# The attention's output product moves to another accumulator bank, and the attention's end is reordered, in a decoder layer on one core

## The chip, the core and the metric

The kernel runs on one core of one Trainium2 chip. A core has a matrix engine (TensorE, "PE" in the rows, with its weight loads as "PEld"), a vector engine (VectorE, "DVE"), a scalar engine (ScalarE, "ACT"), a general one (GpSimd, "POOL") and a queue that mostly starts DMAs (SyncE, "SP"). Each works through its own list of instructions in order, and they meet at semaphores. TensorE writes only into PSUM, which has eight banks of 128 partitions by 512 fp32 numbers; here each bank is a named buffer, `bank0` to `bank7`. The metric is the device time of one execution in microseconds (us); lower is better.

## What is computed

One layer of a decoder in fp32 on x of 4 sequences, 512 tokens and 512 channels: x plus attention of its layer norm, then x plus a product with a context quantised to fp8 steps, then x plus a mixture of experts with one shared expert.

```python
x = x + attention(layernorm(x), wq, wk, wv, wo)   # 32 heads of 64, 8 key heads, rotary, causal softmax
x = x + cross(layernorm(x), ctx)                  # both rounded to e4m3 steps, einsum 'emk,enk->emn'
x = x + moe(layernorm(x), Wg, W1, W3, W2, sw1, sw3, sw2)  # 8 experts, top 1, capacity 256, plus a shared one
```

The matrix products run in fp32 accuracy as three products of a high and a low part (`three`: high times high, high times low, low times high).

## The kernel before

The first two thirds of the time are one loop, `for h in range(NH + 7)`, that every engine runs in its own version. NH is 128: 32 units (4 batches times 8 key groups) of 4 heads. In what follows a step is one pass of this loop, and the number behind a helper is the head it works on. In step h TensorE does, in this order: `scores(h, 3)` and `scores(h, 2)`; two thirds of the step's `project` (the query, key and value products of two units later, into banks 6 and 7); `weigh(h - 3)` (turned weights times values, into bank 5); `turn_p(h - 2, 0)` into bank 2; `scores(h, 1)`; `turn_p(h - 2, 1)` into bank 3; in every fourth step `turn_v` (four small transposes); `scores(h, 0)`; `turn_p(h - 2, 2)` into bank 4; the last third of `project`; and `attn_out(h - 7)`, the product of one finished token tile of the attention with wo, six matmuls into bank 5. `turn_p` is the transpose of the softmax weights P. It fills banks 2, 3 and 4, and each of these is read twice: ScalarE rounds it to the high part PTh (`pt_hi`, L887), then VectorE subtracts that to get the low part PTl (`pt_lo`, L1260).

Bank 5 has two users. `weigh` leaves its sum there; ScalarE copies the lower half out (`lower_out`, Otmp, L881) and VectorE adds the two halves (`join`, Opair, L1254). After that `attn_out` may write the bank. VectorE then adds the result to X (`attn_out` on VectorE, L1269), and the next `weigh` waits for this addition (`v_x`). The rule stands in `wait_bank5`.

VectorE's step is: `inverse_sums(h - 1)` (L1208); in some steps one or two extras (maxima of the context at L1292, quantisation steps, the low part of new weights); `masked(h, 3)` and `masked(h, 2)`, which scale and mask 512 and 384 columns of scores (L1219); a key or value piece; `masked(h, 1)`; `join(h - 3)`; `pt_lo(h - 2, 0)`; `masked(h, 0)`; `pt_lo(h - 2, 1)` and `pt_lo(h - 2, 2)`; a rotary product in most steps (L1232); and the addition for `attn_out(h - 7)` at the very end. ScalarE does the exponentials (L875), `lower_out`, `pt_hi` and `pair`; GpSimd divides the weights by their sums (L1660) and makes low parts.

From step SIDE = NH - 11 = 117 on, the work of the next stages is laid in between: a table made by `slots()` gives for each slot number s a list of stages (`plan(s, stage, b, i)` for batch b and tile i). Slots -44 to -9 lie in steps 117 to 134, two in a step; slots -8, -7 and -6 behind the loop; and slots from -5 on in front of the matmuls of the feed-forward part, `ffn(x, k)` with x = 0 to 7 for the shared expert and k = 0 to 7, so that slot 8x + k - 5 comes before `ffn(x, k)`. From `attn_out(117)` on the bank is 7 in place of 5. The stages of a batch run: statistics (`stats2`), scale and bias (`norm2`), a normed copy (`look`), its maxima (`peaks`), `scales`, `scaled`, rounding on VectorE and GpSimd (`cross_round`), transpose (`cross_turn`), product (`cross_product`), then statistics, norm and transpose again (`stats3`, `rstd3`, `norm3`, `route_turn`), and `logits`, `choose` and `place`. The feed-forward weights come as pieces of 256 KB through a ring of six buffers RW; `split_piece` splits each into high and low. Behind the loop `wait_attention` makes an engine wait until the whole attention is done. It stands before the load of the router's weights (Graw) and of two small tables, before the clearing of the tiles Gh and Gl made from them, and before the first `ffn`.

## Time and profile before

| | us |
|---|---|
| median of three runs | 1531.93 (1531.92 to 1536.74) |
| the profiled execution | 1532.62 |
| its span, first to last instruction | 1530.8 |
| mean granted TensorE clock | 0.990 of full speed |

Busy time of the engines over the span: TensorE 1437.9 us (94%), VectorE 1147.5 (75%), GpSimd 1027.0 (67%), ScalarE 984.9 (64%). The sum of a busy engine's rows can exceed the time, because a matmul's end is modelled and overlaps the next one's start; so what a wait costs TensorE is read here from one start to the next. A matmul of 512 columns starts 0.23 us after the one before it when nothing is waited for. Step h = 8 of the attention's loop starts at 98.9 us, step 50 at 408.0, step 120 at 951.6 and step 127 at 1012.5; the first matmul of the feed-forward part is at 1049.0.

### The profile page before, as it was taken

The page shows a single profiled execution, that of the slowest core. Times are in us where ns is not written, and L with a number is a line of the kernel's source. Part 1 is how long each engine was busy: PE and PEld are TensorE (multiplying, and loading weights), DVE is VectorE, ACT ScalarE, POOL GpSimd, SP SyncE. Part 2 cuts the span into 40 slices and gives each one's busy share as a digit, 9 for nine tenths or more (in the row PEclk, how much of TensorE's full clock was granted, in tenths as well). Part 3 has the DMA queues.
Part 4 walks back from the last instruction along what each step waited for, and adds up shares of the span by engine and source line. Part 5 has one row for each costly group of instructions (what it writes and reads, how often), then busy time and mean ns, then how long its engine had stood idle before and what let it go on. Part 6 is the DMA issues. An engine that isn't in the chain of part 4 may idle for free.

```text
span 1530.8 us, 26938 instructions
## 1 busy us (share of the span) xinstructions
PE 1437.9 (94%) x8617; PEld 1259.0 (82%) x8617; DVE 1147.5 (75%) x2820; ACT 984.9 (64%) x2509; POOL 1027.0 (67%) x1043
## 2 busy tenths in 40 slices
PE   5899999999999999999999999897898999999997
PEld 3778888888878888778888888776787888999996
DVE  7678888887887887887888788787565754677773
ACT  4687786777776887878878787756141412555562
POOL 3787888888877788888898888644404131366663
PEclk9999999999999999999999999999999999999998
DMA  6445454334322424334234342504111011587772
GB/s 209 116 122 166 124 147 134 87 111 124 84 80 63 112 75 128 88 83 123 73 113 126 82 132 66 169 1 147 43 35 49 22 43 39 170 267 236 253 244 80
DMA packets 108620, 174.74 MB, mean 114 GB/s; under 512 B 20936, under 2 KB 42696, under 8 KB 108480
## 3 DMA queue, kind: packets, MB, share of 16 engines
q1 hardware_dynamic: 104448, 160.51, 36.0%
q0 software_dynamic: 3840, 12.25, 2.1%
q8 instruction: 70, 1.15, 0.3%
q14 instruction: 70, 0.57, 0.1%
q10 hardware_dynamic: 192, 0.26, 0.1%
HBM read 94.05 MB, written 33.18 MB: 83 GB/s over the span
## 4 chain that ended last, share of the span: by engine, by line
PE 66%; ACT 12%; DVE 11%; issue 5%; DMA 2%; POOL 2%; SPq 1%; DVEq 0%; POOLq 0%; ACTq 0%
PE bank L484 15%; PE bank L486 14%; PE bank L485 14%; PE bank L536 5%; ACT P L875 5%; PE bank L551 4%; PE bank L552 3%; PE bank L502 3%; PE bank L503 3%; DVE P L1219 2%; ACT PTh L887 2%; PE bank L476 2%; ACT Otmp L881 2%; DVE PTl L1260 1%; DVE Opair L1254 1%
## 5 line engine op out<-in xcount | busy, mean ns | idle before, releaser
L875 ACT ACTIVATE P<-P,mn 128x512 f32<-128x512 f32 (+3 forms) x512 | 284.5, 557 | 206.9 <-DVE mn L1219 203.1
L1660 POOL TENSOR_TENSOR P<-P,ri 128x128 f32<-128x128 f32 (+3 forms) x512 | 360.7, 737 | 30.7 <-DVE ri L1208 30.7
L1219 DVE CUSTOM_DVE_ANT_0 P<-bank,mask 128x512 f32<-128x512 f32 (+3 forms) x512 | 236.6, 480 | 84.3 <-PE bank L503 82.8
L1260 DVE TENSOR_TENSOR PTl<-bank,PTh 128x512 fp32r<-128x512 f32 (+1 forms) x384 | 229.8, 599 | 34.1 <-ACT PTh L887 31.1
L536 PE MATMUL bank<-ident,P 128*128 128x128 f32 x1280 | 202.6, 273 | 2.5 <-POOL P L1660 2.5
L887 ACT ACTIVATE PTh<-bank 128x512 fp32r<-128x512 f32 (+1 forms) x384 | 198.1, 517 | 3.9 <-PE bank L536 1.0
L502 PE MATMUL bank<-KT,QT 128*128 128x256 f32 (+2 forms) x512 | 188.1, 368 | 6.4 <-DVE mn L1219 6.4
L484 PE MATMUL bank<-XT,Wh 128*128 128x512 f32 x384 | 163.8, 427 | 8.1 <-DVE XT L1190 3.5
L503 PE MATMUL bank<-KT,QT 128*128 128x256 f32 (+2 forms) x512 | 166.0, 324 | 0.0
L551 PE MATMUL bank<-PTh,VS 128*128 128x256 f32 (+2 forms) x512 | 161.1, 326 | 5.2 <-DVE X L1269 2.4
L552 PE MATMUL bank<-PTl,VS 128*128 128x256 f32 (+2 forms) x512 | 154.5, 324 | 0.0
L486 PE MATMUL bank<-XT,Wl 128*128 128x512 f32 x384 | 152.9, 398 | 0.0
L485 PE MATMUL bank<-XT,Wh 128*128 128x512 f32 x384 | 152.6, 397 | 0.0
L536 PEld LDWEIGHTS bank<-ident,P 128*128 128x128 f32 x1280 | 150.1, 141 | 3.0 <-POOL P L1660 3.0
L1698 POOL TENSOR_TENSOR OTl<-Opair,OTh 128x512 fp32r<-128x512 f32 x64 | 83.6, 1306 | 94.7 <-ACT OTh L958 93.9
L484 PE MATMUL bank<-Oh,OTh 128*128 128x512 f32 x256 | 106.0, 414 | 20.9 <-DVE Opair L1254 15.5
L1254 DVE TENSOR_TENSOR Opair<-bank,Otmp 64x512 f32<-64x512 f32 x128 | 87.4, 683 | 39.8 <-ACT Otmp L881 38.5
L502 PEld LDWEIGHTS bank<-KT,QT 128*128 128x128 f32 x512 | 96.8, 189 | 21.2 <-DVE mn L1219 8.9
L1011 ACT ACTIVATE hm<-bank 128x256 f32<-128x256 f32 x96 | 36.4, 379 | 117.8 <-PE bank L486 117.0
L551 PEld LDWEIGHTS bank<-PTh,VS 128*128 128x128 f32 x512 | 96.2, 188 | 19.4 <-issue 6.7
L503 PEld LDWEIGHTS bank<-KT,QT 128*128 128x128 f32 x512 | 97.5, 190 | 10.5
L552 PEld LDWEIGHTS bank<-PTl,VS 128*128 128x128 f32 x512 | 96.1, 188 | 10.0
(225 smaller groups left out, 4090.2 us busy)
## 6 DMA issues: line engine op xcount, KB each, us to landing
RW<-in_wf SPq DMA_DIRECT2D x153, 256.0 KB, 3.4
QT<-qh SPq DMA_DIRECT2D x256, 64.0 KB, 2.0
QT<-ql SPq DMA_DIRECT2D x252, 64.0 KB, 2.0
Oraw<-in_wo SPq DMA_DIRECT2D x16, 512.0 KB, 4.8
KT<-KT SPq DMA_DIRECT2D x32, 256.0 KB, 3.0
Wraw<-in_wqkv SPq DMA_DIRECT2D x9, 768.0 KB, 4.7
xnx<-in_ctx SPq DMA_DIRECT2D x24, 256.0 KB, 3.5
saved<-Wh SPq DMA_DIRECT2D x7, 768.0 KB, 3.5
```

Source lines behind the costliest of these rows:

```text
L484: e.matmul(ps, lh, rh, start=start, stop=False)
L485: e.matmul(ps, lh, rl, start=False, stop=False)
L486: return e.matmul(ps, ll, rh, start=False, stop=stop)
L502: e.matmul(ps[:, 0:k], lhs, KT[:, u % 2, 0, 0:k], start=True, stop=False)
L503: e.matmul(ps[:, 0:k], lhs, KT[:, u % 2, 1, 0:k], start=False, stop=True).then_inc(p_s, 1)
L536: last = e.transpose(ps[:, tokens(m)], src, ident[:, :])
L551: e.matmul(ps[:, q:512], lhs, pt_of(PTh, kb), start=kb == 0, stop=False)
L552: last = e.matmul(ps[:, q:512], lhs, pt_of(PTl, kb), start=False, stop=kb == 3)
L875: e.activation(pq, pq, ACT.Exp, bias=mn[:, z, qb:qb + 1], scale=-1.0, accum_out=rs[:, z, qb:qb + 1]).then_inc(a_exp, 1)
L1219: e.tensor_tensor_reduce(P[:, z, off[qb]:off[qb] + k], bank[n % 2][:, 0:k], mask[:, 512 - k:512], -0.125, BIG, ALU.add, ALU.min, mn[:, z, ...
L1260: e.tensor_tensor(pt_part(PTl, part), bank[2 + part][:, 0:128 * n].rearrange("p (m n) -> p m n", n=128), pt_part(PTh, part).bitcast(F32), ...
L1660: e.tensor_tensor(pq, pq, ri[:, z, qb:qb + 1].to_broadcast([128, n]), ALU.mult).then_inc(g_norm, 1)
```

## The change

Three things are changed.

1. The bank of `attn_out`. `attn_out(n)` for n below 117 writes bank 2, which it shares with `turn_p(., 0)`, in place of bank 5. TensorE waits there for both readers of `turn_p(h - 2, 0)` in that bank. The addition to X moves on VectorE from the end of step h to step h + 1, behind `masked(h + 1, 3)` and `masked(h + 1, 2)`, and `turn_p(h - 1, 0)` in step h + 1 waits for it. `weigh` now waits for `join` alone. The first transposes of batches 2 and 3 (`first_turn` in steps 52 to 59) move from bank 2 to bank 5. From `attn_out(124)` on the outputs alternate between banks 7 and 2.
2. The table. Batch 1's statistics go to slots -44 to -38, its scale to a short start on VectorE and 14 small instructions on GpSimd, its `look`, `peaks`, `scales`, `scaled` and rounding up to six slots earlier, its `cross_turn` and `cross_product` one slot earlier. Batch 0's `logits`, `choose` and `place` go from slots -2, 0 and 3 to -6, -4 and -2. GpSimd's part of `place` is a stage of its own, `scatter`, in the old slots.
3. The end of the loop. The router's weights and tables are loaded in step 125, their tiles are made in steps 128 to 130, the pieces' loads start a step earlier, eleven pieces are split in steps 128 to 133 in place of eight in steps 131 to 134, an activation that brings in the Silu table runs in step 129, and most uses of `wait_attention` become waits for just the bank or tile that is needed.

```diff
+    plan(-6, "logits", 0)
+    plan(-4, "choose", 0)
+    plan(-2, "place", 0)
+    plan(3, "scatter", 0)
+    for i in range(TB):
+        plan(-44 + 2 * i, "stats2", 1, i)
+        plan(-14 + i, "look", 1, i)
+        at = (-4, -3, -1, 1)[i]
+        plan(at, "cross_round", 1, i)
+        plan((-1, 0, 1, 3)[i], "cross_turn", 1, i)
...
+        pieces_at = {NH: 2, NH + 1: 2, NH + 2: 1, NH + 3: 2, NH + 4: 2, NH + 5: 2}
...
+        def out_bank(n):
+            return bank[2 if n < NH - 11 or n >= NH - 4 and n % 2 else 7]
...
-        def wait_bank5(need, h, user):
-            if user == "attn_out":
-                need.wait_ge(a_tmp, h - 2)
-                need.wait_ge(v_join, h - 2)
-            elif h < 8 or h - 8 >= NH - 11:
-                need.wait_ge(a_tmp, h - 3)
-                need.wait_ge(v_join, h - 3)
-            else:
-                need.wait_ge(v_x, h - 7)
+        def wait_bank5(need, h):
+            if 53 <= h < 61:
+                wait_xt(need, h - 44)
+            else:
+                need.wait_ge(a_tmp, h - 3)
+                need.wait_ge(v_join, h - 3)
...
             def turn_p(h, part):
-                if part == 0 and 51 <= h < 59:
-                    wait_xt(need, h - 42)
+                if part == 0 and 0 <= h - 6 < NH - 11:
+                    need.wait_ge(v_x, h - 5)
...
             def attn_out(n):
-                ps = bank[7 if late else 5][:, :]
+                ps = out_bank(n)[:, :]
                 if not late:
-                    wait_bank5(need, n + 7, "attn_out")
+                    need.wait_ge(a_pt, 3 * (n + 5) + 1)
+                    need.wait_ge(v_pt, 3 * (n + 5) + 1)
                 elif n == NH - 11:
                     wait_part(need, NU - 1, 2)
-                else:
+                elif n <= NH - 4:
                     need.wait_ge(v_x, n)
+                else:
+                    need.wait_ge(a_pt, 3 * NH)
+                    need.wait_ge(v_pt, 3 * NH)
+                    need.wait_ge(v_x, n - 1)
...
                     if x == 0 and k < 3:
-                        wait_attention(need)
+                        need.wait_ge(a_pt, 3 * NH)
+                        need.wait_ge(v_pt, 3 * NH)
+                        need.wait_ge(a_tmp, NH)
+                        need.wait_ge(v_join, NH)
+                        if k == 2:
+                            need.wait_ge(v_x, NH)
...
# VectorE's loop
                     masked(h, 3)
                     masked(h, 2)
+                if 0 <= h - 8 < NH - 11:
+                    attn_out(h - 8)
...
-                if 0 <= h - 7 < NH:
+                if NH - 11 <= h - 7 < NH:
                     attn_out(h - 7)
...
# the DMA queue's loop
-                if h == NH - 2:
+                if h == NH - 3:
+                    need.wait_ge(g_bq, len(jobs))
+                    e.dma_start(Graw[:, :, :], wg_in).then_inc(d_k, 16)
+                    e.dma_start(rank[:, :], rank_in).then_inc(d_k, 16)
+                    e.dma_start(tri[:, :], tri_in).then_inc(d_k, 16)
                     for _ in range(NR):
                         load_piece()
```

How the moved instructions stand can be seen in three places. The line numbers behind L are those of each version of the file. On TensorE, first, the end of a step in the middle of the attention, before (`ident,P` into bank 4 is `turn_p(h - 2, 2)`, `XT0,Wh` is `project`, `Oh,OTh` is `attn_out`, `KT,QT` the next step's scores):

```order
L536 MATMUL bank4<-ident,P 128x128 x2
L484 MATMUL bank6<-XT0,Wh 128x512
L485 MATMUL bank6<-XT0,Wh 128x512
L486 MATMUL bank6<-XT0,Wl 128x512
L484 MATMUL bank5<-Oh,OTh 128x512 [waits v_join,a_tmp]
L485 MATMUL bank5<-Ol,OTh 128x512
```

The same place after:

```order
L563 MATMUL bank4<-ident,P 128x128 x2
L511 MATMUL bank6<-XT0,Wh 128x512
L512 MATMUL bank6<-XT0,Wh 128x512
L513 MATMUL bank6<-XT0,Wl 128x512
L511 MATMUL bank2<-Oh,OTh 128x512 [waits v_pt,a_pt]
L512 MATMUL bank2<-Ol,OTh 128x512
```

Nothing has moved in TensorE's list here: the bank and the semaphores are other ones. On VectorE, one step from the join on, before (`Opair` is `join`, `PTl` is `pt_lo`, the ISA rows with `mask` are `masked`, `X<-X,bank5` is the addition):

```order
L1254 TENSOR_TENSOR Opair<-bank5,Otmp 64x512 [waits a_tmp]
L1260 TENSOR_TENSOR PTl<-bank2,PTh 128x512 [waits p_pv,a_pt]
L1219 ISA P,mn<-bank1,mask 128x128 [waits p_s]
L1219 ISA mn 128x1
L1260 TENSOR_TENSOR PTl<-bank3,PTh 128x4x128 [waits a_pt]
L1260 TENSOR_TENSOR PTl<-bank4,PTh 128x2x128 [waits a_pt]
L1269 TENSOR_TENSOR X<-X,bank5 128x512 [waits v_x,p_ao]
L1208 RECIPROCAL ri<-rs 128x4 [waits a_exp]
L1292 TENSOR_REDUCE wam<-xnx 128x4 [waits d_by0]
L1219 ISA P,mn<-bank0,mask 128x512 [waits p_pt,p_s]
L1219 ISA mn 128x1
L1219 ISA P,mn<-bank1,mask 128x384 [waits p_s]
```

And after:

```order
L1294 TENSOR_TENSOR Opair<-bank5,Otmp 64x512 [waits a_tmp]
L1300 TENSOR_TENSOR PTl<-bank2,PTh 128x512 [waits p_pv,a_pt]
L1259 ISA P,mn<-bank1,mask 128x128 [waits p_s]
L1259 ISA mn 128x1
L1300 TENSOR_TENSOR PTl<-bank3,PTh 128x4x128 [waits a_pt]
L1300 TENSOR_TENSOR PTl<-bank4,PTh 128x2x128 [waits a_pt]
L1248 RECIPROCAL ri<-rs 128x4 [waits a_exp]
L1332 TENSOR_REDUCE wam<-xnx 128x4 [waits d_by0]
L1259 ISA P,mn<-bank0,mask 128x512 [waits p_pt,p_s]
L1259 ISA mn 128x1
L1259 ISA P,mn<-bank1,mask 128x384 [waits p_s]
L1259 ISA mn 128x1
```

The addition has left the place behind the third `pt_lo` (it now follows the last row shown), and `join` and the first `pt_lo` stand in the same order as before. On the DMA queue, at the attention's end, before (`RW` are the feed-forward pieces, `Graw`, `rank` and `tri` the router's weights and tables):

```order
L1980 DMA RW<-in_wf 128x512 [waits v_piece,a_piece]
L1980 DMA RW<-in_wf 128x512 [waits g_piece,a_piece]
L2083 DMA Graw<-in_wg 128x32 [waits v_x,g_o,a_o,p_ao]
L2084 DMA rank<-in_rank 128x8
L2085 DMA tri<-in_tri 128x128
```

And after:

```order
L2132 DMA Graw<-in_wg 128x32 [waits g_bq]
L2133 DMA rank<-in_rank 128x8
L2134 DMA tri<-in_tri 128x128
L2035 DMA RW<-in_wf 128x512 [waits d_keep]
L2035 DMA RW<-in_wf 128x512 x5
```

Before, the three tables are loaded behind fourteen pieces and the wait for the whole attention; now they are ahead of the first piece.

## Rows read from the trace of the kernel before

**Rows 1.** The page's head and its busy line of TensorE

```profile
span 1530.8 us, 26938 instructions
...
PE 1437.9 (94%) x8617; PEld 1259.0 (82%) x8617; DVE 1147.5 (75%) x2820; ACT 984.9 (64%) x2509; POOL 1027.0 (67%) x1043
```

**Rows 2.** Windows: stretch, length, busy us (count) by engine, granted clock, DMA share, GB/s

```profile
600.00:950.00 350.00, 339.23 (x1919) 289.59 (x1917) 284.13 (x756) 280.94 (x754) 305.63 (x322) 1.00 0.37 98
...
1020.00:1050.00 30.00, 23.44 (x126) 19.15 (x126) 25.49 (x58) 14.38 (x27) 11.00 (x10) 0.94 0.27 84
1050.00:1083.00 33.00, 24.53 (x161) 22.65 (x160) 24.18 (x51) 20.49 (x49) 17.98 (x22) 0.90 0.33 95
```

**Rows 3.** Waits, 105 to 960 us: us in total, times, longest

```profile
PE bank L484 <- DVE Opair L1254: 13.7, 26, 1.2
...
PE bank L502 <- DVE mn L1219: 2.9, 4, 1.2
...
PE bank L551 <- DVE X L1269: 1.2, 2, 0.9
```

**Rows 4.** Timeline of TensorE, steps 49 and 50: start us, us, instruction

```profile
404.37 0.60 PE L536 MATMUL bank<-ident,P 128*128 128x128 f32 x4
404.72 0.36 PE L502 MATMUL bank<-KT,QT 128*128 128x256 f32 x1
...
406.62 0.39 PE L484 MATMUL bank<-Oh,OTh 128*128 128x512 f32 x1
...
411.84 0.36 PE L502 MATMUL bank<-KT,QT 128*128 128x256 f32 x1
...
413.74 0.39 PE L484 MATMUL bank<-Oh,OTh 128*128 128x512 f32 x1
```

**Rows 5.** Timeline of VectorE, the same two steps

```profile
403.12 0.09 DVE L1219 DVE_READ_ACCUMULATOR2_ANT mn<- 128x1 f32 x1
...
405.24 0.42 DVE L1219 CUSTOM_DVE_ANT_0 P<-bank,mask 128x256 f32<-128x256 f32 x1 [1.52 <-PE bank L503]
...
405.59 0.68 DVE L1254 TENSOR_TENSOR Opair<-bank,Otmp 64x512 f32<-64x512 f32 x1
406.20 0.67 DVE L1260 TENSOR_TENSOR PTl<-bank,PTh 128x512 fp32r<-128x512 f32 x1
...
412.82 0.68 DVE L1254 TENSOR_TENSOR Opair<-bank,Otmp 64x512 f32<-64x512 f32 x1
413.54 0.69 DVE L1260 TENSOR_TENSOR PTl<-bank,PTh 128x512 fp32r<-128x512 f32 x1
```

**Rows 6.** Timeline of TensorE, step 109, the wait in front of attn_out

```profile
874.42 0.40 PE L486 MATMUL bank<-XT,Wl 128*128 128x512 f32 x1
875.79 0.47 PE L484 MATMUL bank<-Oh,OTh 128*128 128x512 f32 x1 [0.97 <-DVE Opair L1254]
```

**Rows 7.** Timeline of VectorE, step 109

```profile
874.96 0.68 DVE L1254 TENSOR_TENSOR Opair<-bank,Otmp 64x512 f32<-64x512 f32 x1 [1.16 <-ACT Otmp L881]
875.58 0.69 DVE L1260 TENSOR_TENSOR PTl<-bank,PTh 128x512 fp32r<-128x512 f32 x1
```

**Rows 8.** Timeline of TensorE from the last attn_outs to batch 1's product

```profile
1042.11 0.50 PE L484 MATMUL bank<-Oh,OTh 128*128 128x512 f32 x1 [1.11 <-DVE X L1269]
1046.05 0.50 PE L484 MATMUL bank<-Oh,OTh 128*128 128x512 f32 x1 [2.28 <-DVE X L1269]
1049.01 0.36 PE L484 MATMUL bank<-XT,Uh 128*128 128x256 f32 x1 [1.31 <-issue]
...
1059.22 0.47 PE L484 MATMUL bank<-XT,Gh 128*128 128x512 f32 x1 [1.52 <-issue]
...
1073.61 1.08 PE L476 MATMUL bank<-ident,work 128*128 128x128 f32 x4 [5.48 <-POOL work L1707]
...
1080.43 0.47 PE L484 MATMUL bank<-XT,YT 128*128 128x512 f32 x1 [1.47 <-ACT YT L964]
```

**Rows 9.** Timeline of ScalarE, the router's tables and the wait for their load

```profile
1057.17 0.23 ACT L1113 ACTIVATE Gh<-Graw 128x32 fp32r<-128x32 f32 x1 [2.19 <-DMA tri<-in_tri]
...
1058.42 1.28 ACT L1011 ACT_TABLE_LOAD   x1
```

145 lines of the change are left out of this document (84 added, 61 removed).

## Prediction

> **What bounds the kernel now.** I read the head of the page first [rows 1]: TensorE is busy for 94% of the span, and no other engine for more than 75%. So a change can win only where TensorE waits, and it loses wherever it makes TensorE wait more. The windows say where it waits [rows 2]: in the attention's loop 339.2 of 350 us are busy, while in the 63 us from 1020 to 1083, where the attention ends and the feed-forward part begins, only 48.0 are. The waits of the loop [rows 3] name what the change aims at: `attn_out` (L484 with Opair as releaser) waits for the join in front of bank 5. The profile gives 13.7 us in 26 pieces, and leaves out what the modelled ends of the matmuls cover. From start to start (the start of `attn_out`'s first matmul, less the start of the matmul before it, less 0.23 us) I get 21.3 us over steps 8 to 116, counting every step. Smaller waits of the same stretch are the scores' wait for a mask and `weigh`'s wait for the addition to X, 4.1 us in the profile [rows 3] and 5.5 from start to start.
>
> **The new place of attn_out, step by step.** The change takes away the wait for the join, and puts a wait for both readers of bank 2 in its place. The second of these is `pt_lo(h - 2, 0)`, and on VectorE that stands directly behind the join. So the new release comes later than the old one, by one VectorE instruction, in every step. What that costs is the question, and a step without any lag shows it. In step 49 the join starts at 405.59 and the `pt_lo` at 406.20 with 0.67 [rows 5]: it ends at 406.87. TensorE starts 0.15 us after such an end (step 109: join 874.96 + 0.68 = 875.64, `attn_out` 875.79 [rows 6, 7]; with this 0.15 the join's ends give every wait of the 21.3 us within 0.02). So `attn_out` could start at 407.02, and it started at 406.62 [rows 4]: a wait of 0.40 in a step that had none. In step 50 it is 413.54 + 0.69 + 0.15 = 414.38 against 413.74 [rows 4, 5]: 0.64. The larger value is that of the steps whose join goes to the upper half of Opair, where neither join nor `pt_lo` overlaps its predecessor (0.72 from start to start, not 0.61).
>
> Can this wait shrink, once TensorE is later? No: its chain begins on TensorE. `scores(h, 1)` starts at 404.72, VectorE stands idle 1.52 us for it and starts the mask at 405.24, then come join, `pt_lo` and `attn_out` [rows 4, 5]. From these scores to `attn_out` TensorE has 1.90 us of work, the chain takes 2.30 to 2.54. A later TensorE moves both ends. Only the fourth kind of step, where `turn_v` puts 0.6 us more work in between, has 0.64 - 0.60 = 0.04 left. For the four kinds I take 0.04, 0.39, 0.64 and 0.50 (the last kind was 0.38 in clean steps and more behind extras), 42.4 us over the 109 steps.
>
> Where VectorE or ScalarE lag, the wait is longer. If `pt_lo` ended in each step where it ended before, the waits would sum to 79.6 us; in step 109 that is 875.58 + 0.69 + 0.15 - 874.65 = 1.77, where 1.14 was waited before. But two things relieve VectorE: the masks come 0.6 us earlier, as the addition no longer stands ahead of them, and each step leaves it at least the 0.4 above. So I take for each step the larger of its floor and its old wait: 49.0 us. **Term 1**: 49.0 - 21.3 = +27.7, from +21.1 (floors alone) to +58.3 (every end as before).
>
> **Term 2**, restarts: behind a wait the second matmul follows 0.31 us after the first in place of 0.23. Some 82 steps of 109 now wait where 45 did: 37 x 0.08 = +3.0.
>
> **Term 3**, waits that go: `weigh` for the addition and the scores for a mask that now comes earlier, -5.5 (0 to -8).
>
> **Term 4**, the addition behind the masks. Now `turn_p(h - 2, 0)` waits for it. The masks and the addition together end where the two masks ended before; in step 49 that is 403.12 + 0.09 = 403.21, plus 0.15, and `turn_p` starts at 404.37 [rows 4, 5], so 1.0 us is free. In about half of the steps, behind extras, nothing was free or up to half a microsecond too little (23.8 us of shortfall over 112 steps). Nearly all of it disappears because TensorE comes 0.4 to 0.8 us later from the step before. Were the wait of term 1 not there, it would be paid here. The first transposes in bank 5 put the same kind of wait in front of `weigh` in eight steps. Together +1 (0 to +5).
>
> **Term 5**, steps 117 to 123: four more statistics of 0.87 us each stand between join and `pt_lo`, and the old loop through bank 5 (weigh, join, attn_out, addition) is cut short in steps that have no `project` to hide anything. +2 (-3 to +6).
>
> **Term 6**, the end, is the gain. The outputs of tiles 126 and 127 waited for the addition before them, the single bank 7, and the first `ffn` for the last one: 1.20, 2.45 and 1.37 us from start to start [rows 8]. Two banks and the finer wait take these: -5.0. The router's product waited 1.5 us at 1059.22, for tiles whose tables were loaded behind the whole attention, which also held ScalarE for 2.19 us [rows 8, 9]; both loads now stand in step 125, and the Silu table's 1.28 us come early: -1.5. Batch 1's chain from `look` to `cross_turn` kept TensorE for 5.64 us at 1073.61, and 1.86 at 1080.43 [rows 8]. Behind the first it ran at the lower of its two clock levels, 1.2 GHz (24 matmuls 0.10 us late each, granted clock 0.90 of full in this window [rows 2]), another 2.4. With the chain six slots earlier and its product one slot earlier all of that should go: -9.9. New waits: `place` comes two slots behind `choose` in place of three, while VectorE's part of `choose` took 3.4 us, and the splits of the pieces fall on a VectorE that is 25.5 of 30 us busy there [rows 2]: +2.4. Sum -14 (-5 to -19).
>
> **The sum** is 27.7 + 3.0 - 5.5 + 1 + 2 - 14 = +14.2 us, on the profiled execution's 1532.62: 1546.8. That execution is 0.7 above the median of the runs, so I predict 1546.
>
> **Rules of the skill.** The gap that the change aims at is the same one in many steps, on the engine that should be saturated [rows 3]. The Trainium skill (Perfetto Trace Analysis, Optimization Strategy) says that such consistent bubbles can mean that there isn't enough PSUM for the next tile. By that rule another bank removes them, -21.3 in place of +27.7; the rows speak against it, since the bank that is given is free later than the old one. The Trainium skill also knows (TensorE: Matmul & The Clock Gate, A second HAM failure mode: psum-queue depth-cycling) that small idles between groups of matmuls, with banks cycled, can make the clock swing between its levels. The window from 600 to 950 us had waits up to 1.2 us, and its granted clock was 1.00 [rows 2, 3], so this trace doesn't show it.
>
> **The rivals.** *Not slower, because the bubbles go.* If VectorE's lag, and not the chain from the scores, sets join and `pt_lo` in nearly all steps, its 0.6 us of relief moves both ahead, and `attn_out` finds bank 2 free. Then terms 1 and 2 are -21.3 and -3, term 3 stays, term 4 is 0: 1532 - 21 - 3 - 5.5 + 2 - 14 = 1491. For it: half of the old waits are behind extras. Against it: the idle 1.52 us in front of the mask [rows 5], which says that VectorE waits for TensorE there. It decides where the floor falls under some 0.05 us a step; at half the floor the change would be about even. *Every `pt_lo` as late as before.* The relief goes nowhere, since ScalarE, busy without a gap in the lagging steps, sets the ends: term 1 is +58.3, and the sum +44.8, 1577. For it: in step 109 the join waited 1.16 us for ScalarE [rows 7]. *The end does not gain* because another wait stands behind each of the named ones: 1532.62 + 28.2 = 1561. *The clock swings*: six matmuls of `attn_out` at half rate in 82 steps, 6 x 0.2 x 82 = +98, about 1644. *Even*: the floor at its low end with all of the end's gain, 21.1 + 3 - 8 - 3 - 19 = -6, and somewhat more: 1527 to 1536.
>
> **How the numbers follow.** My forecast 0.60 (its own range 1532 to 1572), the bubbles go 0.14, every `pt_lo` as before 0.14, no gain at the end 0.05, even 0.05, the clock 0.02. A measurement of this kernel can tell about 0.3% from no change, 1527.3 to 1536.5. Faster is the first rival, 0.14. Same is the even case and the low edge of the forecast, 0.05 + 0.05 = 0.10. Slower is the rest, 0.76. The range leaves out the first rival, the clock, and the edges: 1527 to 1580.
>
> **What would show it.** If I am right, `attn_out` waits in three of four steps, released by PTl and not by Opair, for 45 to 60 us in all; a step of the early attention lasts 7.5 to 7.8 us where it lasted 7.12; there is no wait of `weigh` for X; `turn_p` hardly waits for X; and the first feed-forward matmul comes some 20 us later than 1049, followed by no gap of 5 us. I am wrong if step 50 or a step like it still takes 7.12 us, if the large wait is that of `turn_p` for X, or if the end of the kernel, from the first `ffn` on, isn't 8 us or more shorter than before.

## The result and the profile after

The change makes the kernel slower: 1584.49 us, the median of four runs (1582.49 to 1585.53), against 1532.66 (1531.92 to 1536.74) of the kernel before on the same chip. The ratio is 1.0335, with a 95% interval of 1.032 to 1.035. The prediction was 1546, with a range that ended at 1580: the sign is right, the size is not. The loss is 51.8 us where 14 were forecast. The profiled execution after spans 1580.4 us, 49.6 more than before.

The page's head and its line of TensorE, and two of its groups (the line of the operation, what it writes and reads, count | busy, mean ns | idle before it and the main releaser). They answer to [rows 1]:

```profile
span 1580.4 us, 27143 instructions
...
PE 1457.1 (92%) x8617; PEld 1260.5 (80%) x8617; DVE 1172.5 (74%) x2810; ACT 986.3 (62%) x2510; POOL 1026.7 (65%) x1057
...
L563 PE MATMUL bank<-ident,P 128*128 128x128 f32 x1280 | 205.0, 275 | 17.1 <-DVE X L1309 13.7
...
L511 PE MATMUL bank<-Oh,OTh 128*128 128x512 f32 x256 | 111.3, 435 | 43.6 <-DVE PTl L1300 41.7
```

In the changed kernel L511 is the first product of a group of three (L484 before), L563 is `turn_p` (L536), L578 `weigh` (L551), L1259 the mask (L1219), L1294 the join (L1254), L1300 `pt_lo` (L1260), L1309 the addition to X (L1269), L918 ScalarE's copy for the join (L881), L924 `pt_hi` (L887). TensorE does the same 8617 products. What is new are two waits: `attn_out` for PTl, 41.7 us, and `turn_p` for X, 13.7 us.

Where the 49.6 us lie, from start to start as in the prediction: 44.2 in steps 8 to 116 (830.9 us before, 875.1 after), 10.2 in steps 117 to 126 (82.7, 92.9), and -4.2 from step 127 to the end (518.3, 514.1), with -0.6 ahead of step 8. The waits of TensorE in steps 8 to 116, counted in the same way:

| in front of | before | after | forecast change | measured |
|---|---|---|---|---|
| attn_out (terms 1, 2) | 23.8 | 54.5 | +30.7 | +30.7 |
| scores and weigh (term 3) | 8.9 | 3.9 | -5.5 | -5.0 |
| turn_p (term 4) | 1.4 | 20.0 | +1 | +18.6 |

Here is `attn_out`'s wait in the profile, over the same steps. It answers to [rows 3]:

```profile
PE bank L511 <- DVE PTl L1300: 31.5, 79, 1.8
PE bank L563 <- DVE X L1309: 12.6, 14, 3.9
```

And here is one step of it, on TensorE and then on VectorE: step 50, the one whose wait the prediction worked out as 0.64 [rows 4, 5].

```profile
429.76 0.36 PE L529 MATMUL bank<-KT,QT 128*128 128x256 f32 x1
...
431.43 0.40 PE L513 MATMUL bank<-XT,Wl 128*128 128x512 f32 x1
432.30 0.47 PE L511 MATMUL bank<-Oh,OTh 128*128 128x512 f32 x1 [0.47 <-DVE PTl L1300]
```

```profile
430.28 0.42 DVE L1259 CUSTOM_DVE_ANT_0 P<-bank,mask 128x256 f32<-128x256 f32 x1 [1.32 <-PE bank L530]
...
430.75 0.69 DVE L1294 TENSOR_TENSOR Opair<-bank,Otmp 64x512 f32<-64x512 f32 x1
431.46 0.69 DVE L1300 TENSOR_TENSOR PTl<-bank,PTh 128x512 fp32r<-128x512 f32 x1
```

From `scores(h, 1)` at 429.76 to `attn_out` at 432.30 are 2.54 us, as the prediction's chain had it. VectorE still stands idle 1.32 us for the scores. TensorE starts 0.15 us after `pt_lo`'s end (432.15), and waits 432.30 - 431.43 - 0.23 = 0.64.

The other wait at its largest is in step 114. On VectorE, GpSimd and TensorE, in this order:

```profile
944.93 5.12 DVE L1366 TENSOR_SCALAR Zb<-Zb 128x512 f32<-128x512 f32 x1
949.98 0.68 DVE L1259 CUSTOM_DVE_ANT_0 P<-bank,mask 128x512 f32<-128x512 f32 x1
...
951.07 0.68 DVE L1309 TENSOR_TENSOR X<-X,bank 128x512 f32<-128x512 f32 x1
```

```profile
943.06 2.76 POOL L1701 TENSOR_TENSOR P<-P,ri 128x128 f32<-128x128 f32 x4
945.77 1.29 POOL L1784 TENSOR_TENSOR xnx<-xnx,Zb 128x512 f32<-128x512 f32 x1
947.02 2.75 POOL L1701 TENSOR_TENSOR P<-P,ri 128x128 f32<-128x128 f32 x4
949.73 1.45 POOL L1728 TENSOR_TENSOR KT<-kt,KT 64x512 fp32r<-64x512 f32 x1
```

```profile
951.89 0.63 PE L563 MATMUL bank<-ident,P 128*128 128x128 f32 x4 [3.86 <-DVE X L1309]
```

The operation on Zb is an extra that stands in front of the two large masks. It takes 0.40 us when nothing disturbs it. Here it took 5.12, while GpSimd worked without a gap. Masks, addition and `turn_p` stand behind it in a row.

The second largest is in step 79, where another extra, the look for a maximum, waits on VectorE for ScalarE. Before the change only masks stood behind it.

```profile
666.16 0.69 DVE L1346 TENSOR_REDUCE aam<-Wraw 128x4 f32<-128x512 f32 x1 [3.44 <-ACT Wraw L939]
```

```profile
668.68 0.63 PE L563 MATMUL bank<-ident,P 128*128 128x128 f32 x4 [2.84 <-DVE X L1309]
```

### The profile page after: what moved, and what is told of

Its sections match the earlier page's. It is cut to its first block, busy times and chain, and to the rows that moved or that the text cites. A ratio compares the mean times of both kernels' runs of the same rounds, so it can differ in the third digit from the quotient of the medians.

```text
span 1580.4 us, 27143 instructions
## 1 busy us (share of the span) xinstructions
PE 1457.1 (92%) x8617; PEld 1260.5 (80%) x8617; DVE 1172.5 (74%) x2810; ACT 986.3 (62%) x2510; POOL 1026.7 (65%) x1057
## 4 chain that ended last, share of the span: by engine, by line
PE 67%; DVE 16%; issue 7%; ACT 6%; DMA 2%; POOL 1%; SPq 1%; DVEq 0%; POOLq 0%; ACTq 0%
PE bank L511 16%; PE bank L512 14%; PE bank L513 14%; PE bank L563 5%; DVE PTl L1300 4%; PE bank L578 4%; PE bank L579 4%; PE bank L529 4%; PE bank L530 4%; DVE Opair L1294 3%; DVE P L1259 2%; PE bank L503 2%; ACT P L912 2%; ACT PTh L924 1%; DMA Oraw<-in_wo 1%
## 5 line engine op out<-in xcount | busy, mean ns | idle before, releaser
L1259 DVE CUSTOM_DVE_ANT_0 P<-bank,mask 128x512 f32<-128x512 f32 (+3 forms) x512 | 238.1, 483 | 140.8 <-PE bank L530 138.1
L1300 DVE TENSOR_TENSOR PTl<-bank,PTh 128x512 fp32r<-128x512 f32 (+1 forms) x384 | 228.7, 596 | 33.9 <-ACT PTh L924 31.6
L563 PE MATMUL bank<-ident,P 128*128 128x128 f32 x1280 | 205.0, 275 | 17.1 <-DVE X L1309 13.7
L924 ACT ACTIVATE PTh<-bank 128x512 fp32r<-128x512 f32 (+1 forms) x384 | 196.8, 514 | 3.6 <-PE bank L563 0.5
L511 PE MATMUL bank<-XT,Wh 128*128 128x512 f32 x384 | 163.7, 426 | 5.4 <-DVE XT L1230 2.9
L563 PEld LDWEIGHTS bank<-ident,P 128*128 128x128 f32 x1280 | 149.2, 142 | 22.5 <-POOL P L1701 14.5
L578 PE MATMUL bank<-PTh,VS 128*128 128x256 f32 (+2 forms) x512 | 160.3, 324 | 6.5 <-DVE PTl L1300 2.8
L511 PE MATMUL bank<-Oh,OTh 128*128 128x512 f32 x256 | 111.3, 435 | 43.6 <-DVE PTl L1300 41.7
L511 PEld LDWEIGHTS bank<-Oh,OTh 128*128 128x128 f32 x256 | 48.4, 189 | 92.5 <-ACT PTh L924 50.2
L578 PEld LDWEIGHTS bank<-PTh,VS 128*128 128x128 f32 x512 | 96.2, 188 | 17.8 <-issue 5.0
L918 ACT ACTIVATE Otmp<-bank 64x512 f32<-64x512 f32 x128 | 76.3, 596 | 49.2 <-PE bank L579 47.7
L530 PEld LDWEIGHTS bank<-KT,QT 128*128 128x128 f32 x512 | 98.1, 192 | 10.2
```

What stands on the lines that cost most here:

```text
L511: e.matmul(ps, lh, rh, start=start, stop=False)
L530: e.matmul(ps[:, 0:k], lhs, KT[:, u % 2, 1, 0:k], start=False, stop=True).then_inc(p_s, 1)
L563: last = e.transpose(ps[:, tokens(m)], src, ident[:, :])
L578: e.matmul(ps[:, q:512], lhs, pt_of(PTh, kb), start=kb == 0, stop=False)
L1259: e.tensor_tensor_reduce(P[:, z, off[qb]:off[qb] + k], bank[n % 2][:, 0:k], mask[:, 512 - k:512], -0.125, BIG, ALU.add, ALU.min, mn[:, z, ...
L1300: e.tensor_tensor(pt_part(PTl, part), bank[2 + part][:, 0:128 * n].rearrange("p (m n) -> p m n", n=128), pt_part(PTh, part).bitcast(F32), ...
```

## Experiments: which part costs

In the diffs, lines with - are of the kernel that is named and lines with + of the experiment. Every ratio is against runs of the kernel before on the same chip; compare these, and not the last microsecond of the medians.

**The new end alone.** The changed kernel with the bank part undone:

```diff
-            return bank[2 if n < NH - 11 or n >= NH - 4 and n % 2 else 7]
+            return bank[5 if n < NH - 11 else 2 if n >= NH - 4 and n % 2 else 7]
...
-                if 0 <= h - 8 < NH - 11:
-                    attn_out(h - 8)
...
-                if NH - 11 <= h - 7 < NH:
+                if 0 <= h - 7 < NH:
                     attn_out(h - 7)
```

> The changed kernel with the bank part undone: attn_out goes to bank 5 again behind the join, its addition stands at the end of the step, weigh waits for the addition, the first transposes use bank 2. The reordered end stays whole. Theory (the loss up to step 117, 43.7 us between the two traces, is all of the new bank and the moved addition; the end has its own balance): the time is 1532.7 plus what the end brings. If the 10.1 us lost in steps 117 to 127 are the end's own statistics and constants, 1532.7 + 10.1 - 4.2 = 1538.6; if they follow from the bank part, 1532.7 - 4.2 = 1528.5. By the prediction's terms 5 and 6 (-12) it would be 1520.7. Rival (the end's new order, by its other places on VectorE and ScalarE, costs the attention itself): step 117 starts well after the 929.8 us of before, and the time is over 1545.

Measured: 1531.7 us, ratio 0.9991 (0.9981 to 1.0001). Any gain or cost of the new end lies within the interval. Steps 117 to 126 take 87.4 us against 82.7, so 4.7 of the 10.2 us lost there are the end's own, and what comes later gives back as much.

**The bank part alone.** The kernel before with bank 2, the addition behind the masks, `turn_p`'s wait, and the first transposes in bank 5:

```diff
-                ps = bank[7 if late else 5][:, :]
+                ps = bank[7 if late else 2][:, :]
...
                     masked(h, 2)
+                if 0 <= h - 8 < NH - 11:
+                    attn_out(h - 8)
```

> The kernel before with the bank part alone: attn_out up to output 116 in bank 2, its addition behind the next step's two large masks, turn_p waiting for it, the first transposes in bank 5. Everything at the end as before. Theory (the bank part is the loss): step 117 starts some 43.7 us later than 929.8, and the time is 1532.7 + 43.7 = 1576; with the 10.1 us of steps 117 to 127, if these are its as well, 1586. Rival (half or more of the loss belongs to the end's order): below 1560.

Measured: 1584.5 us, ratio 1.0316 (1.0291 to 1.0342). This is the whole loss. Its trace has 46.1 us more than before in steps 8 to 116, and 5.5 more in steps 117 to 126 (88.2 us). With the 4.7 above this makes the 10.2.

## Experiments: bank, order and addition

Five kernels move three things one at a time: the addition's place, the place of `pt_lo(h - 2, 0)` on VectorE (in front of the join or behind it), and the place of `pt_hi(h - 2, 0)` on ScalarE (in front of the copy for the join or behind it). All have the new end and bank 2.

**The addition last.** In the changed kernel:

```diff
-                if 0 <= h - 8 < NH - 11:
-                    attn_out(h - 8)
...
-                if NH - 11 <= h - 7 < NH:
+                if 0 <= h - 7 < NH:
                     attn_out(h - 7)
```

> The changed kernel, attn_out in bank 2, but with its addition to X at the end of the step on VectorE, where the kernel before has it. Theory (turn_p's 20.0 us of wait come from the place behind the extras and the two masks, and nothing else hangs on it): turn_p's waits fall to under 2 us, attn_out's stay at 50 to 58, the scores wait some 3 to 4 us more for a mask, and the time is 1584.5 - 18.6 + 4 = 1570. Rival (the masks' 0.6 us of earliness is what keeps the join and pt_lo from coming still later): what turn_p gives back attn_out takes, its waits are 70 us or more, and the time is within 5 us of 1584.5.

**pt_lo first.** In the changed kernel:

```diff
-                if 0 <= h - 3 < NH:
-                    join(h - 3)
...
                 if 0 <= h - 2 < NH:
                     pt_lo(h - 2, 0)
+                if 0 <= h - 3 < NH:
+                    join(h - 3)
```

> The changed kernel with one swap on VectorE: pt_lo(h - 2, 0), which frees bank 2 for attn_out, stands in front of join(h - 3) and no longer behind it. pt_hi of the same bank ends 0.08 to 0.2 us behind the join's start in the trace after, so pt_lo can start some 0.6 us earlier in clean steps. Theory (the chain scores, mask, join, pt_lo is the 54.4 us of attn_out's waits, and the join is its superfluous link): the waits of attn_out fall to 10 to 20 us; some of it comes back in front of turn_p, since TensorE is earlier there against an addition that is not (up to the 23.8 us of shortfall that the prediction worked out): 1584.5 - 39 + 0 to 24 = 1546 to 1570. Rival (ScalarE's half, pt_hi, frees the bank last): the waits stay above 40 us and the time above 1575.

**Both.** The two edits above together.

> Both single edits together: attn_out in bank 2, its addition at the end of the step, and pt_lo(h - 2, 0) in front of join(h - 3). One edit alone gave 4 us, the other 8 us, of the 51. Theory (the two waits stand in for each other: TensorE, the masks and the addition form one loop, and each edit alone only moves the loss to the other wait): together they give far more than 12 us. turn_p waits under 2 us; attn_out's waits over steps 8 to 117 come to 24 (as before) to 45 us (pt_hi stands behind lower_out on ScalarE, 0.6 us, in the steps in which ScalarE lags): 1532 to 1553, likeliest 1540. Rival (bank 2 is too late whatever the order, because turn_p, pt_hi and pt_lo are the longest chain): attn_out's waits stay at 50 or more, and the time is 1565 or more, the sum of the single gains being 1572.

**Both, and pt_hi first on ScalarE.** One more edit, in ScalarE's loop:

```diff
-                if 0 <= h - 3 < NH:
-                    lower_out(h - 3)
...
                 if 0 <= h - 2 < NH:
                     pt_hi(h - 2, 0)
+                if 0 <= h - 3 < NH:
+                    lower_out(h - 3)
```

> The last kernel with one more swap, on ScalarE: pt_hi(h - 2, 0) in front of lower_out(h - 3), the copy that the join needs. Theory (in steps in which ScalarE lags, bank 2 waits for pt_hi behind the copy, 0.6 us): attn_out's waits fall to 8 to 20 us, and the time is 10 to 20 us under the last kernel's, 1520 to 1535, a version that may beat both. Rival (in steps without a lag weigh's result is there before turn_p's, so the swap makes ScalarE wait for turn_p and pushes the exponentials and all behind them by up to 0.5 us): the scores and turn_p wait more, and the time is that of the last kernel or up to 15 us above.

**Both swaps, the addition behind the masks.** The last kernel with

```diff
+                if 0 <= h - 8 < NH - 11:
+                    attn_out(h - 8)
...
-                if 0 <= h - 7 < NH:
+                if NH - 11 <= h - 7 < NH:
                     attn_out(h - 7)
```

> The kernel of the experiment that came back to 1533 (bank 2, both swaps), with one difference: the addition to X stands behind the next step's large masks, as the change has it, and no longer at the end of the step. Theory (with bank 2 free early, the addition's place is what is left of the loss: turn_p must wait for it behind the masks and the extras): attn_out waits 10 to 25 us over steps 8 to 117, turn_p 35 to 42, as with the swap on VectorE alone, and the time is 1562 to 1573. Rival (the swap on ScalarE relieves everything, also what stands behind turn_p, so the addition's place costs little): turn_p waits under 15 us, and the time is 1533 to 1545.

Measured, with the waits over steps 8 to 116 from start to start:

| order of bank 2's release | addition behind the masks | addition last |
|---|---|---|
| as changed | 1584.5 (attn_out 54.5, turn_p 20.0) | 1580.4, ratio 1.0301 (67.3, 1.3) |
| pt_lo first | 1576.0, ratio 1.0274 (24.4, 40.2) | 1586.3, ratio 1.0332 (70.0, 2.2) |
| pt_lo and pt_hi first | 1564.9, ratio 1.0215 (7.5, 43.7) | 1533.0, ratio 0.999 (21.1, 1.5) |

Three of my expectations failed here. For the addition last I expected 1570: the theory that nothing else hangs on its place fell, since `turn_p` gave back 18.7 us and `attn_out` took 12.8 of them, the scores another 3. For both edits together I expected 1540 and got 1586.3, no gain at all. `pt_lo` first missed its range too, 1576.0 where I had expected 1546 to 1570, as `turn_p` took more back than the 24 us that I allowed. The rival that I had named there (bank 2 is too late whatever the order) fell with the next kernel: one swap on ScalarE is worth 53 us, where I had expected 10 to 20.

What was missing in my picture is a ring, a chain of waits that comes back to its own start one step later. These rows are of the kernel with both edits, from step 49 into step 50, on VectorE, ScalarE and TensorE:

```profile
424.31 0.69 DVE L1300 TENSOR_TENSOR PTl<-bank,PTh 128x512 fp32r<-128x512 f32 x1 [0.28 <-ACT PTh L924]
424.91 0.67 DVE L1294 TENSOR_TENSOR Opair<-bank,Otmp 64x512 f32<-64x512 f32 x1
425.51 0.27 DVE L1259 CUSTOM_DVE_ANT_0 P<-bank,mask 128x128 f32<-128x128 f32 x1
...
426.63 0.42 DVE L1300 TENSOR_TENSOR PTl<-bank,PTh 128x256 fp32r<-128x256 f32 x1 [0.23 <-ACT PTh L924]
426.97 0.68 DVE L1272 TENSOR_TENSOR qcs<-bank,rope 128x512 f32<-128x512 f32 x1
427.56 0.68 DVE L1309 TENSOR_TENSOR X<-X,bank 128x512 f32<-128x512 f32 x1
...
428.25 0.66 DVE L1259 CUSTOM_DVE_ANT_0 P<-bank,mask 128x512 f32<-128x512 f32 x1
...
431.64 0.69 DVE L1300 TENSOR_TENSOR PTl<-bank,PTh 128x512 fp32r<-128x512 f32 x1 [0.23 <-ACT PTh L924]
```

```profile
425.83 0.40 ACT L912 ACTIVATE P<-P,mn 128x128 f32<-128x128 f32 x1
...
426.23 0.36 ACT L924 ACTIVATE PTh<-bank 128x256 fp32r<-128x256 f32 x1
428.95 0.72 ACT L912 ACTIVATE P<-P,mn 128x512 f32<-128x512 f32 x1 [2.36 <-DVE mn L1259]
...
429.67 0.60 ACT L912 ACTIVATE P<-P,mn 128x384 f32<-128x384 f32 x1
...
430.39 0.59 ACT L918 ACTIVATE Otmp<-bank 64x512 f32<-64x512 f32 x1
431.01 0.60 ACT L924 ACTIVATE PTh<-bank 128x512 fp32r<-128x512 f32 x1
```

```profile
425.14 0.47 PE L511 MATMUL bank<-Oh,OTh 128*128 128x512 f32 x1
...
426.38 0.40 PE L513 MATMUL bank<-Oh,OTl 128*128 128x512 f32 x1
...
432.48 0.47 PE L511 MATMUL bank<-Oh,OTh 128*128 128x512 f32 x1
```

Read them in order: `pt_lo` for bank 2 at 424.31, the join, the small mask at 425.51, its exponential at 425.83, the third `pt_hi` and the third `pt_lo` at 426.63, the rotary product, the addition at 427.56, the large mask, the exponentials at 428.95 and 429.67, the copy at 430.39, `pt_hi` at 431.01, and `pt_lo` for bank 2 again at 431.64. One round is 7.33 us. TensorE's own work for such a step is 7.12, and it follows the ring: `attn_out` starts at 425.14 and at 432.48, each time 0.14 or 0.15 us behind the end of `pt_lo`. `attn_out` itself is no link of the ring in these rows: its last product starts at 426.38, and the addition starts 1.18 later, directly behind VectorE's own work. The round before, from 416.93 to 424.31, is 7.38 us and runs over four more activations of ScalarE in place of the addition. In the steps in which VectorE has an extra the round holds both the extra and the addition and is longer, as the one from 408.47 to 416.93 us, 8.46, with the low part of new weights in it. Over steps 8 to 49 the four kinds of step take 8.44, 7.38, 7.35 and 7.97 us in the median, against 7.73, 7.12, 7.14 and 7.28 before the change.

This fits the table. The addition is 0.6 us of the round wherever the round passes it, and behind the masks it is out of it; but then `turn_p` waits for an addition that stands behind masks and extras, over 40 us once `attn_out` no longer delays TensorE. With the addition last, `pt_lo` first gains nothing, because it still follows copy and `pt_hi`: it starts 1.25 us behind the copy's start here, and 1.34 behind it (copy, join, `pt_lo`) with the old order. `pt_hi` in front of the copy takes another 0.6 us out of the round, which is then shorter than TensorE's 7.12 (some 6.7 by these rows, an estimate). In bank 5 the round has the same length, as the join follows the copy directly there and needs no `pt_hi`. So a wait in a ring isn't always removed by moving one link; the ring has to become shorter than the bottleneck's own step. That these links bind in every step is not shown, only in the rows above. Here is step 49 of the kernel with both swaps:

```profile
401.95 0.60 ACT L924 ACTIVATE PTh<-bank 128x512 fp32r<-128x512 f32 x1 [0.39 <-PE bank L563]
402.58 0.59 ACT L918 ACTIVATE Otmp<-bank 64x512 f32<-64x512 f32 x1
```

```profile
402.58 0.69 DVE L1300 TENSOR_TENSOR PTl<-bank,PTh 128x512 fp32r<-128x512 f32 x1
403.20 0.68 DVE L1294 TENSOR_TENSOR Opair<-bank,Otmp 64x512 f32<-64x512 f32 x1
```

```profile
403.57 0.39 PE L511 MATMUL bank<-Oh,OTh 128*128 128x512 f32 x1
```

`pt_hi` now waits 0.39 us for TensorE, so ScalarE is no longer late. `pt_lo` ends at 403.27, 0.15 later bank 2 is free, and `attn_out` follows its predecessor without a wait. The copy and the join cost nobody anything, since bank 5 is not needed before the next step's `weigh`.

**The extras behind the addition.** In the changed kernel all of VectorE's extras (weight splits, maxima, looks, the operations on Zb) go from in front of the masks to behind the addition:

```diff
-                if h - 4 in begins:
-                    large_steps_of(begins[h - 4])
...
                 if 0 <= h - 8 < NH - 11:
                     attn_out(h - 8)
...
+                if h - 4 in begins:
+                    large_steps_of(begins[h - 4])
```

> The changed kernel with VectorE's extras (weight splits, maxima, look, the two rounding operations on Zb) moved from in front of the large masks to just behind the addition to X. Theory (turn_p's 20.0 us over steps 8 to 117 come from these extras standing in front of the addition, 5.12 us of one rounding operation among them): turn_p's waits fall to under 6 us. The extras now stand in front of the rest of the step, so part comes back at attn_out, 5 to 13 us: 1572 to 1584, likeliest 1576. Whether the operation on Zb that took 5.12 us is held again tells whether this hangs on its place: if it is held by the instructions that GpSimd runs at that moment, another instance may be held for over 1.5 us or none. Rival (the addition's own 0.68 us and the masks set turn_p's waits in all steps): turn_p still waits 15 us or more, 1584.

Measured: 1578.1 us, ratio 1.028. `turn_p`'s waits over steps 8 to 116 fall from 20.0 to 4.4, so the extras are what they come from. `attn_out`'s grow from 54.5 to 64.7, and steps 117 to 126 take 98.6 us in place of 92.9. An operation on Zb was held again, for 4.10 us in step 113. So moving the extras leads to the other wait once more.

**The held operation.** The changed kernel, with the two operations on Zb walking the tile in another pattern:

```diff
-                e.tensor_scalar(q.bitcast(U32), y.bitcast(U32), 0x7F800000, None, ALU.bitwise_and).then_inc(v_bm, 1)
+                q, y = (v.bitcast(U32).rearrange("p (a b) -> p b a", b=2) for v in (q, y))
+                e.tensor_scalar(q, y, 0x7F800000, None, ALU.bitwise_and).then_inc(v_bm, 1)
...
+                q = q.rearrange("p (a b) -> p b a", b=2)
                 e.tensor_scalar(q, q, 2.0 ** -6, 1.5 * 2.0 ** 20, ALU.max, ALU.mult).then_inc(v_bq, 1)
```

> The changed kernel with the two rounding operations on Zb (TENSOR_SCALAR, 128x512, SBUF to SBUF) reading and writing every second element in two passes of one instruction, the same values by another access pattern. In the traces so far such an operation takes 0.40 us alone, 1.43 to 1.57 when it begins up to 0.1 us behind a GpSimd instruction of 1.3 us, and 5.12 in step 114 of the changed kernel, while GpSimd ran without a gap (6.57 and 4.10 in two other kernels). Theory (the operation needs something that GpSimd holds while it works, and with another pattern it runs in a form that does not): all forty take about the same, 0.6 to 0.8 us, also beside GpSimd, the 5.12 us and turn_p's 4.3 us in step 114 are gone, turn_p's waits over steps 8 to 117 fall from 20 to 14 to 16 us, the time is 1578 to 1582. Rival 1 (the pattern changes nothing in what is held): durations from 0.4 to over 1.4 us spread as before, and one long one where GpSimd runs without a gap. Rival 2 (the long duration has nothing to do with GpSimd, it is a wait for the values that were rounded before): step 114 keeps a wait of some 4 us, whatever the duration shown.

Measured: 1584.7 us, ratio 1.0332. The first rival holds: undisturbed operations still take 0.40 us, those that begin just behind a GpSimd instruction 1.42 to 1.54, and step 114 has 5.07. The pattern changed nothing, not even the undisturbed 0.40, so nothing shows that the operation ran in another form. It shows that the durations repeat. What the two engines share, and why GpSimd let VectorE in after one instruction in most steps but not in step 114, stays open.

## Experiments: the end in parts

**Two banks and finer waits only**, on the kernel before:

```diff
-                ps = bank[7 if late else 5][:, :]
+                ps = out_bank(n)[:, :]
...
-                else:
+                elif n <= NH - 4:
                     need.wait_ge(v_x, n)
+                else:
+                    need.wait_ge(a_pt, 3 * NH)
+                    need.wait_ge(v_pt, 3 * NH)
+                    need.wait_ge(v_x, n - 1)
```

> The kernel before with one part of the reordered end alone: the last outputs alternate between banks 7 and 2, and the first feed-forward products wait for the banks' readers, not for the whole attention. Constants, pieces of the weights and batch 1's chain stay where the kernel before has them. Theory (the 5.0 us of waits in front of outputs 126 and 127 and of the first product are the single bank's): the first feed-forward matmul comes 3 to 5 us before 1049.0, and the time is 1528 to 1530. Rival (another wait stands right behind: weigh of the last heads, or what ScalarE or VectorE still have to do): the first product comes less than 1.5 us earlier, and the time is within 1.5 us of the kernel before.

Measured: 1533.2 us, ratio 0.999 (0.998 to 1.000). The first feed-forward product comes at 1044.0, 5.0 us earlier, as the theory said. Yet the kernel is no faster than its comparison can tell. Most of the gain sits in one wait of the next stretch, TensorE's for the router's product, which was 1.52 [rows 8]:

```profile
1058.74 0.77 PE L488 MATMUL bank<-XT,Gh 128*128 128x512 f32 x1 [6.03 <-issue]
```

ScalarE makes its table only at 1056.69, once the load has landed. Behind this wait TensorE's granted clock is 0.58 from 1056 to 1064 us, where the kernel before had 0.99 from 1049 to 1073 us:

```profile
1056.69 0.23 ACT L1126 ACTIVATE Gh<-Graw 128x32 fp32r<-128x32 f32 x1 [1.41 <-DMA tri<-in_tri]
```

**The same with the constants, the Silu table and the pieces moved too:**

```diff
-                if h > NH + 2:
-                    for _ in range(2):
-                        split_piece(0, pieces.pop(0))
+                for _ in range(pieces_at.get(h, 0)):
+                    split_piece(0, pieces.pop(0))
+                if h == NH + 1:
...
+                    e.activation(Gh[:, :, 0:8], Graw[:, :, :], ACT.Copy).then_inc(a_const, 1)
```

> The kernel before with the new end except batch 1's chain: the two banks and finer waits as in the last experiment, and the router's constants, the Silu table and the first weight pieces moved into steps 125 to 133. In the last experiment the first feed-forward product came 5.0 us earlier (1044.0), and 6.0 us of it went back in one wait, 5.98 us in front of the router's product at 1058.74, whose tables ScalarE loads only then. Theory (the two gains stand one behind the other, and the constants' place sets the second): this wait falls under 1.5 us, the first feed-forward product stays at 1044 to 1047, and the time is 1526 to 1530. Rival (the pieces' splits, now among the last heads, hold up VectorE and ScalarE there): weigh of the last heads waits 4 us more, the first product comes at 1049 or later, and the time is that of before or more. The chain's other place alone would then be what the kernel with the whole new end adds: 4.7 us in steps 117 to 127 by its trace.

Measured: 1531.6 us, ratio 0.9979 (0.9965 to 0.9993), where I had expected 1526 to 1530. The router's wait is gone, but the first product comes at 1052.0. The last heads' `weigh` waits in its place, and this kernel's trace names VectorE's `pt_lo` as what it waits for, as the rival said:

```profile
1037.01 0.77 PE L558 MATMUL bank<-PTh,VS 128*128 128x512 f32 x1 [2.78 <-DVE PTl L1275]
```

**The constants without the pieces.** The last kernel with the pieces put back:

```diff
-                for _ in range(pieces_at.get(h, 0)):
-                    split_piece(0, pieces.pop(0))
+                if h > NH + 2:
+                    for _ in range(2):
+                        split_piece(0, pieces.pop(0))
```

> The kernel before with the two banks and finer waits at the end, and with the router's constants and the Silu table in steps 125 to 133, but with the weight pieces loaded and split where the kernel before does it, and batch 1's chain as before. With the pieces moved as well, weigh of the last heads waited 1.66 and 2.72 us where it waits 0.86 and 0.62 without them and without the constants, and the first feed-forward product came at 1052.0 in place of 1044.0. Theory (these are the pieces' splits on VectorE and ScalarE): the first product comes at 1044 to 1046, the router's product no longer waits 6 us, and the time is 1526 to 1528.5, faster than both kernels by 0.3 to 0.4%. Rival A (the constants' own instructions, 2.2 us on ScalarE and the Silu table, push the last heads): weigh waits as with the pieces, first product 1049 or later, time 1531 or more. Rival B (behind the router's product the chain of batch 1 takes all that is won, since it starts at a time of its own): the wait of 5.64 us in front of its first transposes grows to 9 or more, and the time is within 2 us of the kernel before.

Measured: 1529.4 us, ratio 0.9978 (0.9969 to 0.9987), where I had expected 1526 to 1528.5. The first product comes at 1043.3 and the router doesn't wait. The last heads' `weigh` waits 1.67 and 1.04 us, so of the 4.38 of the last kernel some 1.7 were the pieces'. But a feed-forward product now waits for VectorE, and batch 1's transposes wait 5.68 us as they did before:

```profile
1057.30 0.39 PE L488 MATMUL bank<-XT,Uh 128*128 128x256 f32 x1 [2.49 <-DVE hm L1500]
```

This kernel and the one before it have the lowest ratios of all, 0.9978 and 0.9979. The intervals of both end under 1, so some 0.2% is gained; it is less than the 0.3% that the prediction set as what can be told from no change, and the pieces make no difference that shows.

**The kernel with constants and pieces moved, and the attention of bank 2 with both swaps:**

```diff
-            return bank[5 if n < NH - 11 else 2 if n >= NH - 4 and n % 2 else 7]
+            return bank[2 if n < NH - 11 or n >= NH - 4 and n % 2 else 7]
```

> The attention of the kernel with both swaps (bank 2, addition at the end of the step, pt_hi and pt_lo in front of the copy and the join), with the new end but without batch 1's moved chain. Theory (both parts add up): the attention costs what it costs in the kernel before, within 2 us, and the end gains what the first kernel of this set gains: its time, within 2 us, 1526 to 1530, faster than both kernels. Rival (bank 2 costs the steps 117 to 127 more, by the look of the statistics there): 2 to 5 us above the first kernel of this set.

Measured: 1533.7 us, ratio 1.0001 (0.9988 to 1.0015), where I had expected 1526 to 1530. No gain: with `attn_out` out of bank 5 nothing comes faster than with it there. It is 2.1 us above the kernel that differs from it by the bank and the swaps, which is at the edge of what these runs can tell.

Set side by side by stretches (us), the end reads:

| kernel | steps 117 to 126 | step 127 to first product | from there to the third set's first product (1128.0 before) |
|---|---|---|---|
| before | 82.7 | 36.5 | 79.0 |
| two banks | 82.6 | 31.9 | 85.1 |
| and constants | 83.0 | 31.5 | 82.2 |
| and pieces | 84.2 | 35.6 | 78.3 |
| and batch 1's chain (the whole end) | 87.4 | 36.8 | 73.0 |

Most of what a line wins in one column it loses in another: the sums are 198.2, 199.6, 196.7, 198.1 and 197.1. In the last line twelve router products, 2.8 us of TensorE's work, stand in the second column and no longer in the third. I had costed each named wait as if the work behind it were free to come earlier.

## Why the prediction was wrong, step by step

**Terms 1 and 2, attn_out: right.** 30.7 us against 30.7. The floors for the four kinds of step were 0.04, 0.39, 0.64 and 0.50; in steps 8 to 49 the medians are 0.11, 0.46, 0.71 and 0.46, the restart of 0.07 to 0.08 among them. By kind, the 109 steps wait 3.1, 16.2, 18.8 and 16.4 us: small amounts in three steps of four.

**Term 3: right.** 5.0 us against 5.5. `weigh` doesn't wait for X in the loop any more.

**Term 4, turn_p: mis-sized, +18.6 in place of +1.** This is the step that failed. The prediction had worked out a shortfall of 23.8 us, and then let "nearly all of it" disappear because TensorE comes later from the step before. Two things are wrong with that. The masks in front of the addition wait for scores of the same late TensorE, so the addition comes later too: the very argument ("a later TensorE moves both ends") that term 1 rests on was not applied here. And the extras differ in size: 11 waits of 0.6 us or more make 14.9 of the 20.0 us, among them 3.38 in step 79, where the look waits for ScalarE, and 4.32 in step 114, where the operation on Zb was held. A lateness of 0.4 to 0.8 us covers none of these. The other half of the sentence was right, and more than right: without term 1's wait, 40.2 and 43.7 us are paid here (the kernels with `pt_lo` first).

**Term 5, steps 117 to 126: mis-sized, +10.2 in place of +2.** The bank's part is 5.5, the end's statistics and pieces 4.7. The relief that the prediction set against them (bank 5's shortened loop) is there: `weigh` waited 3.0 us for X in these steps and doesn't any more. What was mis-sized is the cost beside it: `attn_out`'s waits grow from 3.3 to 12.3 us, and `turn_p` waits 2.5 where it waited for nothing.

**Term 6, the end: mis-sized, -4.2 in place of -14**, and the kernel with the new end alone is within 0.1% of the kernel before. Of the named waits only the router's, 1.52, is gone without a successor. The waits of the last outputs and of the first `ffn`, 1.11, 2.28 and 1.31 [rows 8], are down to 0.68, but the last heads' `weigh` waits 1.60 and 2.80 where it waited 0.67. And the largest sub-term, 9.9 us for batch 1's chain, brought next to nothing. These are its waits after the change, 6.78 us against 5.48 + 1.47 = 6.95 [rows 8]:

```profile
1117.86 0.63 PE L503 MATMUL bank<-ident,work 128*128 128x128 f32 x4 [2.06 <-POOL work L1748]
...
1123.51 1.08 PE L503 MATMUL bank<-ident,work 128*128 128x128 f32 x4 [2.14 <-POOL work L1748]
...
1127.16 0.77 PE L511 MATMUL bank<-XT,YT 128*128 128x512 f32 x1 [2.58 <-ACT YT L1005]
```

The clock that should have come back didn't either: 0.61 of full from 1122 to 1129 us, 0.55 in the kernel before from 1073 to 1080. The rounding on GpSimd that the transposes wait for starts at 1113.44, after 3.84 us of waiting for VectorE, which is busy there from 1108.78 on with the split of a piece and with `choose`. The prediction had this as a rival, "the end does not gain", at a chance of 0.05. It should have been the main case for a stretch in which VectorE is busy for 25.49 of 30 us [rows 2]: what leaves one place of its queue stands in another.

**The rivals.** The bubbles didn't go. "Every `pt_lo` as late as before" gave 1577, nearer than my forecast, but by the wrong mechanism: `attn_out` didn't wait 79.6 us but 54.5. The sum that came out is the forecast's term 1, a term 4 of the size of its shortfall, and an end without gain: 1532.6 + 30.7 - 5.0 + 18.6 + 10.2 - 4.2 - 0.6 = 1582.3. The range ended at 1580 because terms 4, 5 and 6 all came out beyond the bounds given for them: +18.6 against 0 to +5, +10.2 against -3 to +6, and -4.2 against -19 to -5.

**What would show it.** The signs named for term 1 are there: 79 waits in the profile for `PTl`, a clean early step of 7.59 or 7.83 us where 7.12 stood. The sign named for being wrong is there too: a large wait of `turn_p` for X, and an end that is shorter by 4.2 us and not by 8.

**The Trainium skill's rule** (Perfetto Trace Analysis, Optimization Strategy), that consistent bubbles can mean too little PSUM, is not borne out by the first form of the change, as the prediction said. The kernel with both swaps doesn't bear it out either: `attn_out` waits 21.1 us in bank 2 and 23.8 in bank 5, and steps 8 to 116 take 831.9 us against 830.9.

## What to carry to other kernels

Before a user is moved to another buffer, draw the whole ring through which its release comes, over all engines, and compare one round with the bottleneck's own work per step: here 7.33 us against 7.12 for one order, and hardly a wait in clean steps for another, with the same instructions. When an operation gets a new waiter, price each thing that stands in front of it in its queue at its worst step, not at its median. And a wait that is removed in a stretch where several engines are busy is a gain only after the next waits in the same stretch have been read against the new times.
